# Windowed attention without mask matmuls: GpSimd zeroes masked exponentials in place, and the orders of all engines are laid out anew

## The reference, cut to what matters

```python
x = x + attn_a(layernorm(x))   # causal linear attention, 16 heads of 16
x = x + ffn(layernorm(x))      # 256 -> 1024 -> 256, ternary weights, relu
x = x + attn_b(layernorm(x))   # windowed softmax attention, 16 query and 4 key heads
x = x + ffn(layernorm(x))
...
# inside attn_b
mask = (pos[:, None] >= pos[None, :]) & (pos[:, None] - pos[None, :] < 64)
scores = einsum('bhqd,bhkd->bhqk', q, k_full) * scale
scores = where(mask, scores, finfo.min)
att = softmax(scores)
y = einsum('bhqk,bhkd->bhqd', att, v_full)
```

## Time and profile before

| what | value |
|---|---|
| median of 3 runs | 3218.69 us (3218.67 to 3219.31) |
| the profiled execution, its own time | 3215.64 us |
| its span from first to last instruction | 3213.6 us |
| mean granted TensorE clock, as a share of 2.4 GHz | 0.988 |
| PE busy | 3043.3 us, 95% |
| DVE busy | 2333.5 us, 73% |
| ACT busy | 1809.6 us, 56% |
| POOL busy | 454.3 us, 14% |

### The profile page before, as it was taken

How to read it: one execution, slowest core, us unless ns; L and a number is a source line. 1 busy time by engine, 2 the same in 40 slices (tenths; PEclk the granted TensorE clock), 3 DMA queues, 4 the chain that set the end, 5 groups by cost and what they waited for, 6 DMA issues and landing times.

```text
span 3213.6 us, 79494 instructions
## 1 busy us (share of the span) xinstructions
PE 3043.3 (95%) x27330; PEld 2423.5 (75%) x27330; DVE 2333.5 (73%) x5990; ACT 1809.6 (56%) x3713; POOL 454.3 (14%) x1036
## 2 busy tenths in 40 slices
PE   3789999999999999999999999999999999999987
PEld 2567887777777777777777778777788777777765
DVE  4468777778777777777777777777877777777754
ACT  1246555665555665555666555666655566555555
POOL 0011111111110111110111111111111011111010
PEclk9889999999999999999999999999999999999999
DMA  1000000000000000000000000000000000000000
GB/s 62 8 10 17 11 5 14 16 16 16 16 2 13 16 16 16 16 2 13 16 16 16 16 2 13 16 16 16 16 16 2 13 16 16 16 16 2 14 10 16
DMA packets 42082, 44.85 MB, mean 14 GB/s; under 512 B 2608, under 2 KB 41392, under 8 KB 42032
## 3 DMA queue, kind: packets, MB, share of 16 engines
q1 hardware_dynamic: 42032, 44.20, 4.5%
HBM read 21.12 MB, written 16.78 MB: 12 GB/s over the span
## 4 chain that ended last, share of the span: by engine, by line
PE 75%; DVE 12%; issue 7%; ACT 4%; POOL 1%; DVEq 0%; ACTq 0%; SPq 0%; DMA 0%; POOLq 0%
PE Q L364 15%; PE HID L414 12%; PE Y L435 12%; PE Q L555 8%; PE Q L823 4%; PE Q L593 4%; PE HID L372 3%; PE Q L588 3%; PE Q L837 2%; PE Q L570 2%; PE Q L606 2%; PE Q L757 2%; ACT f_hh L950 1%; PE Q L844 1%; DVE ff_xn L1297 1%
## 5 line engine op out<-in xcount | busy, mean ns | idle before, releaser
L949 ACT ACTIVATE f_r<-HID,b1c 128x512 f32<-128x512 f32 x512 | 353.0, 689 | 484.9 <-PE HID L414 362.5
L435 PE MATMUL Y<-w2t,f_hh 128*128 128x256 f32 x2048 | 541.0, 297 | 7.7 <-DVE f_hl L1311 5.6
L1311 DVE TENSOR_TENSOR f_hl<-f_r,f_hh 128x512 fp32r<-128x512 f32 x512 | 369.0, 721 | 235.9 <-ACT f_hh L950 235.5
L435 PE MATMUL Y<-w2t,f_hl 128*128 128x256 f32 x2048 | 512.0, 283 | 0.0
L414 PE MATMUL HID<-ff_xh,w1t 128*128 128x512 f32 x1024 | 430.1, 420 | 14.8 <-DVE ff_xl L1303 14.8
L435 PEld LDWEIGHTS Y<-w2t,f_hh 128*128 128x128 f32 x2048 | 388.5, 190 | 59.2 <-issue 25.7
L414 PE MATMUL HID<-ff_xl,w1t 128*128 128x512 f32 x1024 | 407.2, 398 | 0.0
L435 PEld LDWEIGHTS Y<-w2t,f_hl 128*128 128x128 f32 x2048 | 389.9, 190 | 4.1
L950 ACT ACTIVATE f_hh<-HID,b1c 128x512 fp32r<-128x512 f32 x512 | 352.0, 687 | 0.0
L1413 DVE TENSOR_TENSOR a_s<-Q,cst 128x512 f32<-128x512 f32 x512 | 327.8, 681 | 27.6 <-PE Q L555 22.0
L1127 ACT ACTIVATE a_qz<-Q 128x512 f32<-128x512 f32 x512 | 278.8, 602 | 33.4 <-PE Q L762 33.0
(11 more groups left out here) (186 smaller groups left out, 6967.8 us busy)
## 6 DMA issues: line engine op xcount, KB each, us to landing
x<-in_x SPq DMA_DIRECT2D x32, 512.0 KB, 4.3
out<-x SPq DMA_DIRECT2D x32, 512.0 KB, 3.1
b_vm<-b_v SPq DMA_DIRECT2D x64, 96.0 KB, 2.1
a_s<-in_w SPq DMA_DIRECT2D x1, 1024.0 KB, 8.0
a_qz<-in_w SPq DMA_DIRECT2D x1, 1024.0 KB, 10.3
a_s<-in_w_qkv SPq DMA_DIRECT2D x1, 768.0 KB, 4.5
cst<-in_const SPq DMA_DIRECT2D x1, 389.0 KB, 5.2
a_qT<-in_w_b SPq DMA_DIRECT2D x1, 384.0 KB, 5.7
```

The costliest lines, as they stand in the source:

```text
L435: mm = pe.matmul(Y[t // 2][:, (t % 2) * D:(t % 2 + 1) * D], h[:, fb % 2, t * P:(t + 1) * P], w2t[:, fb, :], start=False, stop=(fb == FB - ...
L949: act.activation(f_r[:, fb % 2, :], HID[fb % 2][:], ACT.Relu, bias=b1c[:, fb:fb + 1]).then_inc(f_rr, 1)
L1311: dve.tensor_tensor(f_hl[:, fb % 2, :], f_r[:, fb % 2, :], f_hh[:, fb % 2, :], ALU.subtract).then_inc(f_lo, 1)
```

## The change

The mask matmuls of attention B go away on the unguarded path: the first score matmul of a bank starts it. GpSimd multiplies the exponentials of each block in place by a table of 0 and 1 (`keep`), one 128x512 instruction for each of the two halves, and `numer` waits for these multiplications. The lists of calls of PE, ACT, DVE and POOL are reordered in both phases. The diff, cut to the parts of the computation and to the lists that matter below:

```diff
-_WIDTHS = dict(ident=P, causal=P, heads=HB * HV, parity=2, qodd=P, qfirst=P,
+_WIDTHS = dict(ident=P, causal=P, heads=HB * HV, parity=2, qodd=P, qfirst=P, keep=2 * W,
...
+    put("keep", np.concatenate([odd, (k < W) & (k <= qq)], 1))
...
# PE, scores
-                                         start=False, stop=not guarded, skip_group_check=True)
+                                         start=not guarded and gp == 0, stop=not guarded, skip_group_check=True)
...
-                                pe.wait_ge(b_ex, j * 2 - 1)
-                            mask(bl, 0)
-                            if bl:
                                 pe.wait_ge(b_ex, j * 2)
-                            mask(bl, 1)
...
# PE, numer
-                        pe.wait_ge(b_ex, (b * NBL + bl + 1) * 2)
+                        pe.wait_ge(b_ex if guarded else b_kept, (b * NBL + bl + 1) * 2)
...
# GpSimd, phase 2
+                    def keep(bl):
+
+                        if guarded:
+                            return
+                        for g2 in range(2):
+                            pool.wait_ge(b_ex, (b * NBL + bl) * 2 + g2 + 1)
+                            p = b_p[:, bl % 2, g2, :].rearrange("p (u q) -> p u q", u=8)
+                            kept = C["keep"][:, 0:W] if bl else C["keep"][:, W:]
+                            pool.tensor_tensor(p, p, kept.unsqueeze(1).broadcast_to([P, 8, W]), ALU.mult).then_inc(b_kept, 1)
...
                     sines(0)
+                    own_rstd()
                     sines(1)
-                    own_rstd()
                     sines(2)
+                    keep(0)
+                    keep(1)
+                    keep(2)
                     sines(3)
+                    keep(3)
+                    keep(4)
+                    keep(5)
                     next_rstd()
+                    keep(6)
+                    keep(7)
                     second_rstd()
...
# PE, end of phase 1
                     qkv(s.b, 1, a + 1)
                     qkv(s.b, 2, a + 1)
+                    qkv(s.b, 3, a + 1)
                     down(3)
-                    qkv(s.b, 3, a + 1)
...
# ACT, end of phase 1
+                    raw(s.b, 0)
                     y_hi(3)
                     relu(4)
-                    raw(s.b, 0)
                     raw(s.b, 1)
```

181 lines of the change are left out of this document (91 added, 90 removed).

## The result

The changed kernel takes 3501.6 us (median of 4 runs, 3495.8 to 3513.0) against 3219.0. The ratio is 1.087, 95% interval 1.085 to 1.090: 283 us slower. Forecast were 3275 us and a range to 3340. The direction was right and the size was not; the measured time lies above every case that I had given a chance.

A forecast was written before the change was run, and what follows sets the result against it. PE was taken to bound the kernel nearly everywhere, with DVE from phase 1's end to about `down(1)` of phase 2. Terms -0.84 - 0.85 + 0.2 + 3.0 + 0.3 = +1.8 us per turn, 31 turns, gave 3275 us, range 3185 to 3340.

The forecast's parts named there:

- orders (head, shapes): Reordered lists: 0.85 us per turn saved at the head of phase 2, 0.2 us lost to tile-shape changes.
- masks: Score blocks without mask matmuls: 0.12 us saved in each of seven blocks, 0.84 us per turn.
- keep: GpSimd's multiplications: 3.0 us lost per turn by meeting DVE's instructions, 0.3 us lost at the tail of phase 2.
- The first runs beside `own_apply`: Start of phase 2: the first `keep` instruction beside `own_apply`, which has one operand in SBUF, costs nothing.
- The meeting that I did place there: Second instruction of `keep(0)` and `keep(1)` covers the time when `stack_lo(1)` is due; each meeting costs DVE 0.97 us.
- My 3.0 us: Head of phase 2 to `down(1)`: 3.5 meetings and 0.3 us make DVE 3.7 us later, less 0.7 us slack.
- The clock: a rival without a chance: Masks go but PE's clock falls; waits of some us in 20 were said not to lower it; no chance given.
- The 0.85 us at the head: Head of phase 2: DVE's new list brings `stack_lo(0)` forward and PE follows, 0.85 us saved per turn.
- Small waits, which I can't place: Reordered phase 1: small waits covered by the 0.2 us per turn charged for changes of tile shape.
- The tail of phase 2: From `scores(7)` to `numer(7)`: PE's 3.8 us of work just covers exponential and two multiplications, 3.6 us; 0.3 us lost.
- GpSimd as a link of every block: Rival: a `keep` takes 1.6 us and `numer` waits too, 4.2 us more per turn, 3349 us; chance 0.09.

The follow-up runs named there:

- orders_only: The changed kernel's new orders with the mask matmuls kept and no GpSimd multiplication; ratio 1.018 to the kernel before, 3273 us.
- no_keep: The changed kernel without any GpSimd multiplication, so masked keys stay in the result; 3268 us, ratio 1.017 to the kernel before.
- keep_apart: The changed kernel with full-size GpSimd multiplications on a buffer of their own, `numer` waiting only for the exponentials; 3534 us, ratio 1.099 to the kernel before.
- tiny_keep: The changed kernel with each GpSimd multiplication cut from 512 to 4 elements, all waits staying; 3263 us, ratio 1.014 to the kernel before.
- head_only: The kernel before with only the head of phase 2 reordered on all engines, masks staying; 3243 us.
- keep_after_apply: The changed kernel with one more GpSimd wait, `keep(0)` beginning only when `own_apply` is done; ratio 1.069 to the kernel before, 3443 us.
- masks_out: The kernel before without its mask matmuls, old orders, masked keys staying in the result; ratio 1.000, 3220 us.
- filler_short: The changed kernel with 6 and 5 unneeded 512-column matmuls ahead of `own_norm` and between its halves; 3450 us.
- masks_out_filled: The kernel before without its mask matmuls, with three filling matmuls of 512 columns in the gaps ahead of `scores(0)`; ratio 0.997, 3210 us.
- swap_rotate: The kernel before with one swap in DVE's list, `stack_lo(0)` ahead of `rotate(1)`; 3216 us.
- tail_keep: The kernel before with its orders, masks for blocks 0 to 5 and GpSimd multiplications for blocks 6 and 7 alone; ratio 1.034, 3329 us.

## Why the forecast was off, step by step

The excess per turn is 104.66 - 95.55 = 9.11 us, and 31 x 9.11 = 282 us, the measured difference. It divides as

```
                       forecast    measured   from
orders (head, shapes)    -0.65       +1.72    orders_only - before
masks                    -0.84       -0.29    no_keep - orders_only
keep                     +3.3        +7.68    after - no_keep
sum                      +1.8        +9.11
```

**keep: the failed step.** The mechanism was right in the main: GpSimd and DVE exclude each other, keep_apart and tiny_keep show it. Its price was about right too, where `keep` was there first: a meeting of a `keep` with one DVE instruction of two SBUF operands was priced at 0.97 us, and took 1.56 - 0.68 = 0.88 and 1.59 - 0.685 = 0.9. What failed is the sentence "The first runs beside `own_apply` (one operand in SBUF) and costs nothing." `own_apply` is the costliest meeting of all: its four instructions go from 1.38 to 4.49 us, 3.1 us, with PE directly behind them. I had looked at how many operands it has, and none of my rows showed it beside a GpSimd instruction. That is a price not known, and I put it at nothing without a bound. The same section of the Trainium skill that I had cited (SBUF — State Buffer, Who interferes with whom) names `tensor_scalar` among the instructions that can take both of DVE's port pairs, and says that it then blocks and is blocked like the others. The runs here agree with that sentence, with 1.38 us for the four instructions undisturbed and 4.49 beside four `keep`. I used half of the section. Nor was it a matter of this size alone: in head_only two GpSimd instructions of 160 elements make the same `own_apply` 0.36 us longer.

The meeting that I did place there, `stack_lo(1)`, didn't occur: being behind `own_apply`, it ran undisturbed (0.68 and 0.28 us). In keep_after_apply it did occur, and `stack_lo(1)` took no longer for it: I had charged every meeting to DVE, and there GpSimd paid. Up to `scores(2)` the changed kernel loses 12.10 - 7.36 = 4.74 us against no_keep, and behind it 7.68 - 4.74 = 2.9 us: 1.9 between `scores(3)` and `scores(4)`, where PE waits for `stack_lo(2)`, and 1.0 between `scores(5)` and `scores(6)`, where it waits for `stack_lo(3)`. The first of these I had in the sum; for the meeting of `stack_lo(3)` I had charged nothing. My 3.0 us were meant for everything from `own_apply` to `down(1)`; that the part behind `scores(2)` alone lost as much is chance.

**The clock: a rival without a chance.** I wrote that waits of this size don't lower it. That held for a stretch with the masks in it and 0.94 us without work for PE. Without them a fall follows the same three waits ahead of `scores(0)` in 17 of 25 turns (masks_out), and in most turns of the changed kernel the long waits for `own_apply` come while the clock is low: 0.52 and 0.50 in two stretches. filler_short shows that this costs about 2 us of the turn at least, 1.7 of them among the 4.74 us up to `scores(2)`. It should have had a chance even by my own sum, which has 3 us of new waits in it. The Trainium skill's TensorE: Matmul & The Clock Gate (HAM oscillation — how this bites in real kernels) warns of kernels that fall back to the lower clock because of gaps in TensorE's work. The trace agrees in part: the fall comes among gaps, but those ahead of it, 0.34 to 0.47 us, are far shorter than the 3 to 5 us of that section's kernel.

**The masks: right price, wrong yield.** A block of scores takes 0.43 us as forecast (PE of the changed kernel, 1789.01 - 1788.58):

```profile
1788.58 0.51 PE L764 MATMUL Q<-b_qT,b_kT 64*128 64x256 f32 x4 [0.22 <-ACT b_kT L1116]
1789.01 0.39 PE L437 MATMUL Y<-w2t,f_hh 128*128 128x256 f32 x1
```

But -0.84 per turn became -0.29 in the new orders, where the clock is at the lower level for 1.37 us per turn (no_keep) and not at all with the masks (orders_only), and nothing in the old. In the turns of no_keep whose clock stays up (96.8 us) the saving is 0.5. masks_out_filled has the clock at 1.00 and saves 95.55 - 95.17 = 0.38 us. Even that is half of my term, so some masks stood where PE had time; which, these runs don't say.

**The orders: wrong sign.** The 0.85 us at the head are there (0.75 between `project(3)` and `turn_qk(0,0)`). I had looked only at the waits that the moves take away, and not at what stands behind each instruction that was moved back: `y_hi(3)`, and with it the last projection, `rotate(1)`, and the middle of phase 2; nor at what an instruction would now stand beside, as `sines(3)` beside `own_apply`. And swap_rotate shows that PE at the head can be sooner and still wait for DVE at `turn_qk(1,0)`, which I had read in the earlier trace rows and didn't use here. "Small waits, which I can't place", for which I took a part of 0.2 us, were 1.72 + 0.75 = 2.5 us.

**The tail of phase 2** was charged with 0.3 us and cost nothing in the changed kernel's order. tail_keep shows what the cover is worth there: 3.4 us per turn.

**The rival that came nearest**, GpSimd as a link of every block (3349 us), had the size nearest to the result, but not its cause: in the whole of the changed kernel PE waits for a `keep` twice, 1.8 us in all. What it said of `numer` at the tail is what tail_keep does.

What stays open: how the 7.7 us of `keep` would divide at an undisturbed clock (filler_short gives only a lower bound for the clock, and the filling delays `own_norm` itself); and what makes the clock fall in some turns of masks_out and no_keep and not in others with the same waits.

## What to carry to other kernels

Before work is moved to GpSimd, list every DVE instruction that will stand beside it and look at each kind by itself; an instruction that no row shows beside a long GpSimd one has an unknown price, from nothing to the whole data part, and belongs into the range. Ask which of the two will be there first: here it was the second one that waited. The price is paid where TensorE waits next, and more of it if the clock is low there. Matmuls that seem to be overhead can be what keeps the clock up: replace them by filling first, and see whether their removal saves anything at all.
